# Denominators taken from ones beside x in the weighing products, the division moved behind block turns and onto GpSimd, and the frequency mix one step later

## The reference

```python
h = tok(x)                                    # 32 x 64 x 256
h = h + attn(layernorm(h))
h = h + ffn(layernorm(h))

# attn
q, k, v = xh @ Wq.T, xh @ Wk.T, xh @ Wv.T     # per head of 16
attn = softmax(q k / sqrt(256))               # 64 x 64 per head and batch element
out = (attn @ v) @ W_out.T + b_out
# ffn
y = real(ifft(fft(x) @ w)) + bias             # one 256 x 256 product and a bias
```

## Time and profile before

| | |
|---|---|
| median of the runs | 142.65 us (142.56 to 142.75, 3 runs) |
| the profiled execution | 142.76 us, of which 141.0 us are its span (first to last instruction) |
| busy, share of the span | PE 132.8 us (94%), DVE 111.6 us (79%), POOL 94.7 us (67%), ACT 85.7 us (61%) |
| granted clock of PE | 0.993 of full speed |
| first stage | to about 42.5 us, where the first `scores` start |
| second stage | from there to the end; steps of 5.56 us in its steady part |

### The profile page before, as it was taken

One profiled execution on the slowest core, in us unless ns is written; L12 is line 12 of the kernel. 1 busy time (PEld: TensorE's weight loads), 2 busy tenths in 40 slices (PEclk: granted clock), 3 DMA queues, 4 the chain that ended last, 5 costly groups with the idle time before them and its releaser, 6 DMA issues.

```text
span 141.0 us, 6132 instructions
## 1 busy us (share of the span) xinstructions
PE 132.8 (94%) x2444; PEld 112.4 (80%) x2444; DVE 111.6 (79%) x337; ACT 85.7 (61%) x245; POOL 94.7 (67%) x186
## 2 busy tenths in 40 slices
PE   6879999999999998999999999999999999999861
PEld 2469999999997876978878889889788788788540
DVE  5584596859978578798898898988988988978751
ACT  4374765477878584865947747649558477455110
POOL 3284796996583364677687686786876876773361
PEclk9999999999999999999999999999999999999997
DMA  4678000030000010121312302203113123031102
GB/s 70 157 174 257 14 0 0 0 36 11 2 0 5 5 19 5 19 50 15 63 37 23 60 12 49 56 7 65 46 15 60 37 23 59 6 60 41 38 0 74
DMA packets 24508, 5.89 MB, mean 42 GB/s; under 512 B 20384, under 2 KB 24224, under 8 KB 24480
## 3 DMA queue, kind: packets, MB, share of 16 engines
q1 hardware_dynamic: 24192, 5.37, 18.3%
q10 hardware_dynamic: 288, 0.13, 0.3%
HBM read 2.35 MB, written 2.10 MB: 32 GB/s over the span
## 4 chain that ended last, share of the span: by engine, by line
PE 78%; DVE 7%; POOL 4%; issue 3%; DMA 3%; ACT 1%; SPq 1%; POOLq 0%; DVEq 0%
PE bank L1036 11%; PE bank L954 11%; PE bank L1022 7%; PE bank L1099 6%; PE bank L1075 5%; PE bank L959 5%; PE bank L1080 4%; PE bank L1120 4%; PE bank L1064 3%; DMA wf_raw<-in_W_r 3%; PE bank L1049 2%; PE bank L1133 2%; PE bank L948 2%; PE bank L1103 2%; PE bank L1124 2%
## 5 line engine op out<-in xcount | busy, mean ns | idle before, releaser
L824 DVE TENSOR_REDUCE bank<-bank 128x4 f32<-128x256 f32 x64 | 22.8, 425 | 6.9 <-ACT pT L376 6.5
L376 ACT ACTIVATE pT<-bank 128x256 f32<-128x256 f32 x64 | 19.4, 391 | 2.5 <-PE bank L1049 2.5
L1036 PE MATMUL bank<-qT,xzT 32*128 32x64 f32 x512 | 17.9, 276 | 0.0
L1036 PEld LDWEIGHTS bank<-qT,xzT 32*128 32x128 f32 x512 | 15.7, 186 | 2.7 <-issue 2.7
L695 DVE TENSOR_TENSOR hid_lo<-bank,hid_hi 128x512 fp32r<-128x512 f32 x16 | 11.0, 685 | 7.5 <-ACT bank L344 7.5
L582 POOL TENSOR_TENSOR side_lo<-sideT,side_hi 128x256 fp32r<-128x256 f32 x14 | 10.2, 728 | 8.3 <-ACT sideT L386 8.3
L545 POOL TENSOR_SCALAR xblk<-xh,parity_sb 128x128 f32<-128x128 f32 x32 | 11.5, 372 | 5.9 <-PE bank L1080 4.8
L371 ACT ACTIVATE maxT<-bank 128x128 fp32r<-128x128 f32 x16 | 4.4, 277 | 17.8 <-PE bank L1058 17.8
L593 POOL TENSOR_TENSOR on_lo<-onT,on_hi 128x256 fp32r<-128x256 f32 x14 | 10.3, 737 | 7.1 <-ACT on_hi L390 6.8
L553 POOL TENSOR_TENSOR hb_all<-h_all,bout_bc 128x256 f32<-128x256 f32 x16 | 11.5, 735 | 4.0 <-ACT h_all L348 4.0
L361 ACT ACTIVATE xzT<-bank,parity_sb 128x256 f32<-128x256 f32 x28 | 12.0, 498 | 0.0
(11 more groups left out here) (166 smaller groups left out, 386.8 us busy)
## 6 DMA issues: line engine op xcount, KB each, us to landing
out<-y SPq DMA_DIRECT2D x16, 128.0 KB, 1.7
xblk<-xh SPq DMA_DIRECT2D x32, 32.0 KB, 2.5
wo_raw<-in_W_o SPq DMA_DIRECT2D x1, 512.0 KB, 4.2
wout_raw<-in_W_out SPq DMA_DIRECT2D x1, 256.0 KB, 2.9
fr<-in_wr SPq DMA_DIRECT2D x1, 256.0 KB, 4.3
fi<-in_wi SPq DMA_DIRECT2D x1, 256.0 KB, 4.3
minus_raw<-in_minus_rows SPq DMA_DIRECT2D x1, 128.0 KB, 2.2
bout_bc<-in_b_out SPq DMA_DIRECT2D x1, 128.0 KB, 3.5
```

The lines of the kernel that those rows point to most:

```text
L376: nc.scalar.activation(pT[:, j, :], bank[j][:, D:2 * D], ACT.Exp).then_inc(exp_done, 1)
L824: nc.vector.tensor_reduce(rowmax[:, j, :], bank[j][:, 0:D].rearrange("p (h k) -> p h k", k=TOK), AX_X, ALU.max).then_inc(max_done, 1)
L1036: pe.matmul(bank[j][:, at0:at0 + TOK], xzT[t % 3][rows32, 2 * half + b, :, :].rearrange("p e k -> p (e k)"), qT[t % 3][rows32, half, TOK * ...
```

## The change

The zeros and the separate ones go. `xblk` gets, for each head, 16 columns of x and 16 columns of ones (it is set to 1.0 once, and only the x columns are overwritten); all of x is placed by four DMAs a tile (before two, with two instructions of POOL beside them). A weighing product now has the 64 keys of one head as its rows, so there are 32 of them a tile, of 64 rows by 32 columns of weights, even heads into bank 5 and odd heads into bank 6; the rows 16 to 31 of each block hold the denominator. The four products with `pair_ones` are gone.

DVE transposes both banks' results in one instruction of 512 columns (`invert`), takes the reciprocals, POOL divides (for the last two tiles DVE), and DVE transposes back (`turn_on`). The banks are dealt anew, which brings new waits: the turned x of a tile from 3 on and the turned maxima lie in banks 5 and 6, behind `pv_turned`; the row maxima are written over the scores in banks 0 to 3, so that the next `scores` wait for `max_lo_set`. `mix_freq` and `finish` come one and two steps later than before, `residual` one step later in DVE's queue.

```diff
             def weigh(t):
                 pe.wait_ge(exp_done, QUADS * (t + 1))
-                pe.wait_ge(xblk_same, t + 1)
-                pe.wait_ge(xblk_crossed[t % 2], 32 * (t // 2 + 1))
+                pe.wait_ge(xblk_placed[t % 2], 64 * (t // 2 + 1))
...
-                for j in range(QUADS):
-                    pe.matmul(bank[PV_BANK][32 * j:32 * j + 32, D:2 * D], pair_ones[:], pT[:, j, :], start=True, stop=True)
                 for half in range(HALF):
                     for b in range(2):
                         cols = slice(half * P + TOK * b, half * P + TOK * (b + 1))
-                        for j in range(QUADS):
-                            last = pe.matmul(bank[PV_BANK][32 * j:32 * j + 32, cols],
-                                             xblk[t % 2][:, b, half * P + 32 * j:half * P + 32 * j + 32],
-                                             pT[:, j, cols], start=True, stop=True)
+                        for e in range(2):
+                            for j in range(QUADS):
+                                last = pe.matmul(bank[PV_BANK[e]][32 * j:32 * j + 32, cols],
+                                                 xblk[t % 2][TOK * e:TOK * e + TOK, b, QUADS * half + j, :],
+                                                 pT[TOK * e:TOK * e + TOK, j, cols], start=True, stop=True)
                 last.then_inc(pv_done, 1)
...
+            def invert(t):
+                dve.wait_ge(pv_done, t + 1)
+                if t >= 1:
+                    dve.wait_ge(on_divided, t)
+                nc.vector.transpose(weighedT[:].rearrange("p e c r -> p e (c r)"), weighed[:, :, 0:D]).then_inc(pv_turned, 1)
+                dve.wait_ge(pv_turned, t + 1)
+                nc.vector.reciprocal(inv_sum[:], weighedT[:, :, :, HD]).then_inc(inv_done, 1)
...
+            def turn_on(t):
+                dve.wait_ge(on_divided, t + 1)
...
+                nc.vector.transpose(onT[:].rearrange("p a t -> p (a t)"),
+                                    on_rows[:].rearrange("p c e d -> p (c e d)")).then_inc(on_set, 1)
...
# POOL
+            def divide(t):
+                pool.wait_ge(inv_done, t + 1)
+                nc.gpsimd.tensor_tensor(on_rows[:].rearrange("p c e d -> p e c d"), weighedT[:, :, :, 0:HD],
+                                        inv_sum[:].unsqueeze(3).to_broadcast([P, 2, D // 32, HD]),
+                                        ALU.mult).then_inc(on_divided, 1)
             def step(i):
-                if i + 2 < T:
-                    place_same(i + 2)
...
+                if 2 <= i <= WHOLE_SIDE + 1:
+                    split_side(i - 2)
+                if i < WHOLE_ON:
+                    divide(i)
+                if 1 <= i < T:
+                    add_bias(i - 1)
                 if i < WHOLE_ON:
                     split_on(i)
...
# SP
-                for b in range(2):
-                    e = 1 - b
-                    sp.dma_start(
...
+                for b in range(2):
+                    for e in range(2):
+                        sp.dma_start(xblk[t % 2][TOK * e:TOK * e + TOK, b, :, 0:HD],
+                                     heads[TOK * b:TOK * b + TOK, :, e, :]).then_inc(xblk_placed[t % 2], 16)
...
# PE, new waits
             def scores(t):
+                if t >= 1:
+                    pe.wait_ge(max_lo_set, t)
             def turn_max(t):
...
+                else:
+                    pe.wait_ge(pv_turned, t)
             def mix_freq(t):
...
+                if t < T - 2:
+                    pe.wait_ge(h2_done, t + 2)
             def project(t):
...
+                else:
+                    pe.wait_ge(h2_done, t)
             def turn_x(t):
...
+                if t >= 3:
+                    pe.wait_ge(pv_turned, t - 2)
...
             def step(i):                                     # PE
...
+                if i >= 2:
+                    mix_freq(i - 2)
+                if 0 <= i + 3 < T:
+                    query(i + 3)
                 if i >= 1:
                     turn_side(i - 1)
...
+                if i == T - 1:
                     mix_freq(i - 1)
-                if 0 <= i < T:
+                if i >= 0:
                     project(i)
```

218 lines of the change are left out of this document (101 added, 117 removed).

## The result

The changed kernel takes 152.88 us (median of 4 runs, 152.11 to 156.03) against 142.61 for the kernel before (142.50 to 142.75). The ratio is 1.070, 95% interval 1.063 to 1.077. The prediction was 146.3 us, 143.8 to 150.0: the direction is right, the size is not, and the time is outside the range. The profiled execution took 152.1 us, 150.3 of it span.

What follows compares the result with a forecast made beforehand. PE's queue alone was taken to bound the steady step of 5.57 us. Filling 0.4, twelve steps 0.5, steps 13 and 14 0.3 and tail 2.5 summed to 3.7 more: 146.3 us, range 143.8 to 150.0.

Steps and rivals of the forecast that it cites:

- The steady step: Distance between steps in the steady part: 5.62 us, PE's own work plus two new waits, against 5.57 before.
- The weighing: PE's 64 weighing products on eight tiles: 0.63 us, taken from a like case, bounds 0.56 and 1.12.
- The wait for `x_lo`: PE's query waits for x_lo, behind the turn back in DVE's queue, which waits for POOL: 0.18 us a step.
- The wait for `pv_turned`: PE's transposes of x and maxima wait, after the scores, for DVE's transpose of the weighed rows: 0.31 us a step.
- PE's own step: PE's work in a steady step without waits: 5.56 - 1.02 + 0.63 = 5.17 us.
- The twelve steps: Steady steps from the start of step 1 to 122.28 us: 12 x 0.04 = 0.5 us more.
- rival A: Weighing tiles don't run eight at once or instruction count sets PE's pace: weighing 1.12, step 6.1, total 152.8; chance 0.12.
- Steps 13 and 14: turn_x is gone there but turn_max still waits for DVE's turn: 0.3 us more in all.
- The tail: From DVE's last transpose of weighed rows to the last finish: 8.65 us against 6.11, 2.5 more, as delayed mix and finish pile up.
- Filling: Start of step 1, after POOL's first division and the second weighing: 0.4 us later, bounds -0.1 and +0.6.
- four placing DMAs: Placing x by four DMAs instead of two: no cost, about 11 us of cover against 2.5 to land one.
- DVE's share: DVE's work in a step: a gain of 0.1, about 5.15 us busy, not the bound while the step is longer.

Runs made afterwards that it cites:

- the two shifts of the stream: Changed kernel with 32 or 16 more idle products at its start, moving later PE instructions 64 or 32 places: 152.47 and 154.84 us; 153.93 us profiled (208.48 at clock 0.56).
- the split into 128 products: Changed kernel with each weighing product split into two of 32 columns, 128 a step instead of 64: 187.4 us.
- the run of small products alone: Kernel before the change with each of its 32 weighing products split into two of 32 columns, 64 on four tiles: 144.3 us, no stop.
- without placing: Changed kernel with the placing DMAs of x left out for tiles 2 to 15, so old rows are weighed: 150.41 and 152.51 us.
- with idle products: Changed kernel with 8, 20 and 6 unread products of zeros where PE waits in the last two steps: 150.14 us, ratio 1.051.
- the three runs with the clock up: Changed kernel without placing (150.41, 152.51 us), with idle products (150.14 us), and with the projection put behind the next weighing (146.24 us).
- three orders without the wait: Changed kernel with all of the projection behind the weighing (146.24 us), its last two products there (148.49), or half the keyed scores before the transposes (157.51, 159.66).

## Why the prediction was wrong in size

The prediction had 3.7 us more, the spans show 9.3. Two terms that its sum doesn't have make up most of the difference: the stops of supply, 2.2, and the lower clock of TensorE in the last two steps and the tail, 2.6 to 2.9. The terms that it has come to 0.5 to 0.8 us more than it gave them.

**The steady step: right, by two errors.** 5.62 was said, 5.66 measured. The weighing was mis-sized, 0.63 for 0.79: L1022 was the wrong like case, since it has half as many products. The wait for `x_lo` was put at 0.18 and is 0: the division on POOL was faster than its price, and `x_lo` is done 3.1 us behind the weighing, not 3.5. The wait for `pv_turned` is as worked out: 0.31 said, 0.31 to 0.35 measured. PE's own step is 5.31, not 5.17. (The prediction's own figures, 5.17 and waits of 0.31 and 0.18, give 5.66 and not 5.62; the 0.04 is rounding in its five transposes.) Without the two stops the twelve steps, of which the first is only 5.20, are 0.9 more than before instead of 0.5.

**The twelve steps: the step that failed is one that isn't in the sum.** Of 3.1 us, 2.2 are the two stops. The prediction priced products by their time on PE alone and never asked where instructions come from; rival A spoke of their count, but as PE's pace, and would have put the cost into each weighing (1.12; it is 0.79). Its total of 152.8 is near the measured time by chance. Shown by the two shifts of the stream and by the split into 128 products; the run of small products alone doesn't do it, the late start of the load belongs to it.

**Steps 13 and 14: 0.3 said, 2.2 measured.** The wait for DVE's transpose is 0.28 in step 13 and 0.90 in step 14, where no `scores` are left to cover it; the prediction noted that `turn_x` is gone there and not that `scores` are. With the clock up the two steps are 0.6 (without placing) to 0.9 (with idle products) more than before; the other 1.3 to 1.6 are the lower clock's.

**The tail: 2.5 said, 4.0 measured.** The chain was right: 8.65 was worked out, and in the three runs with the clock up (1.00 all through the tail) it is 8.77 or 8.78. The other 1.3 are the clock, which the sum didn't have: it priced every product of the end at the full clock of the rows before, where it was full until 139.1 of 141.0 us. The four whole products of `mix_freq(14)` took 1.94 there, against 1.10 in the run without placing.

**Filling: 0.4 said, 0.0 measured.** 55.60 against 55.57.

**Terms put at nothing that came to nothing:** four placing DMAs instead of two (leaving them out changed neither the steps nor the stops; those two runs are 0.1 and 2.2 us below the changed kernel, and in the profiled one steps 13, 14 and the tail ran with the clock up), DVE's share, ACT's order.

What stays open is half of the cause: why the load of the next instructions starts so late after PE has passed the last place of its kind. In the steady part of the changed kernel it is 2.9 to 3.0 us after a place in the keyed scores and mostly 0.9 to 1.5 elsewhere, where PE does not stop; in the kernel before it is never over 0.8, in the keyed scores 0.4 to 0.7. Counted in records it is more even: in the steady part the load starts 56 to 129 records behind the place in the changed kernel, and 51 at most in the kernel before. What it waits for no run shows. Nor is it shown why the clock fell behind some of the stops and waits and not behind others.

## What to carry to other kernels

A product that is cheap on TensorE still has to be delivered: count the instructions of an unbroken run of short ones, look in the trace how long before it their load began, and break it with wide products. Cover for a wait isn't free if it alternates wide products with small tiles; here three orders without the wait were 5.56 to 5.70 a step against 5.66 with it. And where a change makes TensorE wait in a stretch that it had filled, price what follows at the lower clock too, as one end of the range: it fell in some executions and not in others.

## What the runs showed of the hardware

- TensorE's instructions come in loads of 16 KB, 256 of them, while the kernel runs. Where PE stood, it went on 2.2 to 3.1 us after the load's start. The weighing and the scores are 192 records in 1.4 us: with a load begun 1.1 us before its first record was wanted PE stood for 1.2 us, with 1.9 to 2.2 us for 0.3 to 1.0, and above 2.7 us never within a block.
- Every idle time of 0.3 us or more within a block of like products at the full clock stands in front of record 193 + 256 k of PE's stream, in all 15 kernels. So a few more instructions in the first microseconds move a stop that comes 80 us later.
- 64 products of 64 columns on eight tiles take 0.79 us, 32 on four tiles 0.56, 64 of half the columns on four tiles 0.67.
- Going from wide products to small tiles or back costs 0.1 to 0.2 us: two transposes take 0.14 to the next start ahead of wide products and 0.31 ahead of small tiles; 16 keyed products 0.46 ahead of small tiles and 0.60 ahead of wide ones.
- A transpose of 512 columns on DVE takes 0.716 us, of 256 columns 0.45. A product of 128x256 on POOL with a broadcast factor takes 0.62, less than the plain one (0.73).
- In the changed kernel's profile the granted clock went to 0.50 2 us after an idle time of 0.9 us, and again behind one of 2.3 us. With idle products in the gaps it stayed at 1.00, and in another run it stayed at 1.00 with the same idle times; these stretches were then 2.6 and 2.9 us shorter.
